# Attention A's relative scores: one read and one write per tile in place of alternating halves

## The chip, the cores and the metric

The kernel runs on one core of a Trainium2 chip. The metric is the device time of one execution in microseconds; the time of a kernel is the median of its runs. The engines are TensorE (PE, with its weight loads PEld), VectorE (DVE), ScalarE (ACT), GpSimd (POOL) and SyncE (SP, which issues nearly all DMAs here). Sixteen DMA engines move what SP issues.

## The reference

Input x is 4 x 2048 x 256, float32. Four layers follow each other: attention A with relative positions, a feed-forward block, causal attention B, and the feed-forward block again. All attention has 16 heads of 16 values. The stage in question is attention A:

```python
content_score = jnp.einsum('bhsp,bhtp->bhst', q + u, k)
pos_score = jnp.einsum('bhsp,htp->bhst', q + v, pos)
pos_score = _relative_shift(pos_score)      # pad a column, reshape to (s+1, s), drop the first row
score = (content_score + pos_score) / jnp.sqrt(jnp.float32(P))
weights = jax.nn.softmax(score, axis=-1)
out = jnp.einsum('bhst,bhtp->bhsp', weights, val)
```

The shift moves row i of the position scores by an amount that depends on i, and takes what lies beyond the diagonal from row i + 1.

## The kernel before

The batches run one after the other in a hardware loop (four passes), and within a pass the stages are separated by meetings of all engines. Attention A works on tiles of 128 query rows by all 2048 key columns: 16 heads x 16 tiles, 256 tiles a pass, 1024 in all. `in_order` unrolls four heads (G = 64 steps) into the body of a loop; all engines run the same steps s, each with its own lead.

The relative shift goes through DRAM. PE computes a tile's position scores into PSUM (`rows_of`, lines 565 and 569, banks of `rg`; `row_tail` for 128 more columns), ACT copies banks 0 to 2 (line 698) and DVE bank 3 and the tail (lines 752, 762) into `rel`, a ring of RING = 4 buffers of 128 x 2176 floats. SP writes the buffer to `rel_rows` in DRAM, a grid with a row pitch of W = 2176 floats (8,704 B), and reads it back with a row pitch of W - 1 floats (8,700 B) into `z`, a ring of 4 buffers of 128 x 2048 floats: each row then starts one float further to the left, which is the shift. DVE adds the content scores of PE (line 591) to z and takes the maxima (`score`, line 717, one instruction for each half of the columns), POOL subtracts the maximum (line 778), PE turns z in four quarters (`turn`, line 598), ACT takes the exponential into `pT` (line 690), and PE multiplies by the values (line 619).

The leads: the position scores of tile s + 9 (R_LEAD), SP's read of tile s + 6 (Z_LEAD), the score of tile s + 4 (C_LEAD), the turn of tile s + 2 (T_LEAD), the values of tile s + 1, all in step s.

SP's step of attention A (`sp_attn_a`, `step`, lines 857 to 869) runs in this order:
- `read_ready(n)`, n = s + 6: wait until PE has turned the last quarter of tile n - 4 (`t_full[3]`), which frees the buffer of z, and until tile n has been written in full (`rel_out`).
- `read_half(n, 0)` (line 822): 128 rows of 4,096 B.
- `write_half(r, 0)` (line 834), r = s + 9: wait for ACT's copy of bank 1, then write 128 rows of 4,096 B.
- `read_half(n, 1)`: 128 rows of 4,096 B.
- `write_half(r, 1)`: wait for DVE's copy of bank 3, ACT's copy of bank 2 and the tail, then write 128 rows of 4,608 B.
- `next_heads`: in some steps the loads of the next heads' q, k, position and value tiles.

Each DMA adds 16 to `rel_in` or `rel_out` of its buffer, and `moved` gives the count at which both halves have landed: 32 a tile. DVE's `score` waits for that count before its first half; ACT and DVE wait for `rel_out` before they copy into a buffer again. No consumer waits for one half alone.

Of the kernel before, what the change touches and what calls it, by code (L numbers as in the profile page):

```python
# [26 lines left out]
P = 128  # L27
# [4 lines left out]
S = 2048  # L32
NT = S // P
# [9 lines left out]
W = S + P  # L43
PAD = 16
FLAT = S * W
RING = 4
# [9 lines left out]
R_ACT = [0, 1, 2]  # L56
R_DVE = 3
R_FIRST = 3
HB = 4
NB = 2  # L60
G = HB * NT
# [5 lines left out]
OB = 4  # L67
# [30 lines left out]
def program(nc, a, out, nb=4, nh=H):  # L98

    ctx = ExitStack()  # L100
    with ctx:
        def sb(name, shape, dt=F32):
            return ctx.enter_context(nc.sbuf_tensor(name, shape, dt))
# [4 lines left out]
        def sem(name):  # L108
            return ctx.enter_context(nc.semaphore(name))
# [8 lines left out]
        rel_d = nc.dram_tensor("rel_rows", (NB, FLAT), F32).ap()  # L118
# [9 lines left out]
        rel = sb("rel", [P, RING, W])  # L128
        z = sb("z", [P, RING, S])
# [125 lines left out]
        rel_out = [sem(f"rel_out{k}") for k in range(RING)]  # L255
        rel_in = [sem(f"rel_in{k}") for k in range(RING)]
        qv_loaded = [sem("qv_loaded0"), sem("qv_loaded1")]
        tail_full = sem("tail_full")
        tail_copied = sem("tail_copied")
# [4 lines left out]
        QK_INC = 16 * 2 * len(GROUP)  # L264
# [6 lines left out]
        def settle(e):  # L271

            e.sem_inc(waited, 1)
# [257 lines left out]
        def in_order(e, b, step):  # L531

            def counts(p):
                return Counts(*(e.snap(b * (nh // HB * per) + p * per)
                                for per in (G, G // OB, 32 * G // RING, HB // NB * QK_INC, HB // NB * 16)))

            with e.Fori(0, 1) as p:
                base = counts(p)
                for s in range(-R_LEAD, 0):
                    step(p, base, s, lambda n: n >= 0)  # L540
            with e.Fori(0, GROUPS - 1) as p:
                base = counts(p)
                for s in range(G):
                    step(p, base, s, lambda n: True)
            with e.Fori(GROUPS - 1, GROUPS) as p:
                base = counts(p)
                for s in range(G):
                    step(p, base, s, lambda n: n < G)

        def moved(base, n):  # L550

            return base.moves + 32 * (n // RING + 1)

        def pe_attn_a(e, b):

# [123 lines left out]
        def act_attn_a(e, b):  # L679

            def step(p, base, s, here):

                r, t = s + R_LEAD, s + T_LEAD
                if here(t):
                    if s >= 0:

                        e.wait_ge(AA["pv_done"], base.tiles + (t - 1))
                    for q in range(4):
                        e.wait_ge(t_full[q], base.tiles + (t + 1))
                        e.activation(pT[:, t % 2, q * CH:(q + 1) * CH], rg[:, T_BANK[q], :], ACT.Exp,  # L690
                                     scale=SCALE).then_inc(p_ready[q], 1)
                if here(r):
                    if s >= 0 or r >= RING:

                        e.wait_ge(rel_out[r % RING], moved(base, r - RING))
                    for c in R_ACT:
                        e.wait_ge(r_full[c], base.tiles + (r + 1))
                        e.activation(rel[:, r % RING, c * CH:(c + 1) * CH], rg[:, R_BANK[c], :],  # L698
                                     ACT.Copy).then_inc(r_copied[c], 1)

            in_order(e, b, step)

        def dve_attn_a(e, b):

            def score(p, base, n, half, first):

                ready, read = (("lo_ready", "lo_read"), ("hi_ready", "hi_read"))[half]
                mx = (mlo, mhi)[half][:, n % 2:n % 2 + 1]
                if half == 0:
                    e.wait_ge(rel_in[n % RING], moved(base, n))  # L710
                    if not first:

                        e.wait_ge(AA["nmax_ready"], base.tiles + (n - 1))
                e.wait_ge(AA[ready], base.tiles + (n + 1))
                settle(e)
                zs = z[:, n % RING, 2 * half * CH:2 * (half + 1) * CH]
                e.tensor_tensor_reduce(out=zs, in0=scf[:, 2 * half * CH:2 * (half + 1) * CH], in1=zs, scale=1.0,  # L717
                                       scalar=-3.0e38, op0=ALU.add, op1=ALU.max, accum_out=mx).then_inc(AA[read], 1)
# [72 lines left out]
        def load_pair(e, q, k, q_src, k_src, h, groups, done):  # L791

            for i in groups:
                load_group(e, q, k, q_src, k_src, h, i, done)

        def load_v(e, h, hd, done):
            e.dma_start(v_s[hd].rearrange("p t w -> p (t w)"),
                        v_d[bass.ds(h, 1)].rearrange("a p w -> (a p) w")).then_inc(done, 16)

        def sp_attn_a(e, b):  # L800

            every = range(len(GROUP))
            load_pair(e, qv_s[0], pos_s[0], qv_d, pos_d, 0, every, qv_loaded[0])
            load_pair(e, qu_s[0], k_s[0], qu_d, k_d, 0, every, AA["qk_loaded0"])
            load_v(e, 0, 0, AA["v_loaded0"])
            load_pair(e, qv_s[1], pos_s[1], qv_d, pos_d, 1, every, qv_loaded[1])

            def read_ready(p, base, n, fresh):

                k = n % RING  # L810
                if not fresh:

                    e.wait_ge(t_full[3], e.snap(base.tiles + (n - RING + 1)))
                    settle(e)
                e.wait_ge(rel_out[k], e.snap(moved(base, n)))
                settle(e)

            def read_half(n, half):

                k, hd, i0, c0 = n % RING, n // NT % NB, n % NT * P, half * S // 2  # L820
                shifted = bass.AP(tensor=rel_d.tensor, offset=hd * FLAT + i0 * W + P - 1 + c0, ap=[[W - 1, P], [1, S // 2]])
                e.dma_start(z[:, k, c0:c0 + S // 2], shifted).then_inc(rel_in[k], 16)

            def write_half(base, n, half):

                k, hd, i0, c0, c1 = n % RING, n // NT % NB, n % NT * P, half * S // 2, (S // 2, W)[half]
                for c in ((R_DVE, R_ACT[-1]) if half else (R_ACT[1],)):
                    e.wait_ge(r_copied[c], e.snap(base.tiles + (n + 1)))
                    settle(e)
                if half:  # L830
                    e.wait_ge(tail_copied, e.snap(base.tiles + (n + 1)))
                    settle(e)
                there = bass.AP(tensor=rel_d.tensor, offset=hd * FLAT + i0 * W + c0, ap=[[W, P], [1, c1 - c0]])
                e.dma_start(there, rel[:, k, c0:c1]).then_inc(rel_out[k], 16)

            def next_heads(p, base, s, final):

                hd, at = s // NT, s % NT
                nxt = (hd + 1) % NB
                if at in (1, 3, 5) and not (final and hd + 1 >= HB):  # L840
                    if at == 1:
                        e.wait_ge(AA["hi_ready"], e.snap(base.tiles + hd * NT + C_LEAD))
                        settle(e)
                    load_pair(e, qu_s[nxt], k_s[nxt], qu_d, k_d, e.snap(p * HB + (hd + 1)), ((at - 1) // 2,),
                              AA[f"qk_loaded{nxt}"])
                if at == 7 and not (final and hd + 1 >= HB):
                    e.wait_ge(AA["pv_done"], e.snap(base.tiles + (hd * NT + V_LEAD)))
                    settle(e)
                    load_v(e, e.snap(p * HB + (hd + 1)), nxt, AA[f"v_loaded{nxt}"])
                if at in (8, 10, 12) and not (final and hd + 2 >= HB):  # L850
                    if at == 8:
                        e.wait_ge(r_full[2], e.snap(base.tiles + (hd + 1) * NT))
                        settle(e)
                    load_pair(e, qv_s[hd % NB], pos_s[hd % NB], qv_d, pos_d, e.snap(p * HB + (hd + 2)), ((at - 8) // 2,),
                              qv_loaded[hd % NB])

            def step(p, base, s, here):

                n, r = s + Z_LEAD, s + R_LEAD
                final = not here(G)  # L860
                if here(n):
                    read_ready(p, base, n, s < 0 and n < RING)
                for half in range(2):
                    if here(n):
                        read_half(n, half)
                    if here(r):
                        write_half(base, r, half)
                if s >= 0:
                    next_heads(p, base, s, final)

            in_order(e, b, step)


# [650 lines left out]
```

## Time and profile before

| | |
|---|---|
| median of 3 runs | 10,336.33 us (10,335.39 to 10,343.65) |
| the profiled execution | 10,338.86 us |
| its span, first to last instruction | 10,337.1 us |
| mean granted TensorE clock | 0.950 |
| PE, PEld busy | 8931.8 us (86%), 5887.2 us (57%) |
| DVE, ACT, POOL busy | 5900.6 us (57%), 5858.0 us (57%), 2783.3 us (27%) |
| moved by DMA | 2543.88 MB in 725600 packets, mean 246 GB/s |

The page also cuts the span into 40 slices with the busy tenths of each engine, the granted clock and the DMA engines' mean busy share, lists the costliest groups of instructions with the idle time ahead of them and what ended it, and lists the DMA issues with their sizes and the median time from issue to landing. A DMA share a little over 1 means that packets of one engine overlap a little. The trace answers the same questions for any stretch of the span.

### The profile page before, as it was taken

The numbers are of one execution on the slowest core, as the hardware profiler recorded it, in microseconds if no ns is written. First come the engines' busy times: TensorE is split into PE (matmuls) and PEld (weight loads), VectorE is DVE, ScalarE is ACT, GpSimd is POOL, SyncE is SP. The second block draws the span as 40 slices with busy tenths as digits, with TensorE's granted clock in tenths as the row PEclk, the third lists the DMA queues.
The fourth block names the chain that finished last, engine by engine and source line by source line (L and its number), as shares of the span: only waits on it lengthen the run. The fifth ranks groups of instructions, "written<-read, shape, count | busy, mean of one in ns | idle before, by whom it ended". The sixth has DMA issues, their size and how long they took to land. (4 is left out here: it accounts for less than half of the span.)

```text
span 10337.1 us, 258386 instructions
## 1 busy us (share of the span) xinstructions
PE 8931.8 (86%) x91488; PEld 5887.2 (57%) x91488; DVE 5900.6 (57%) x12492; ACT 5858.0 (57%) x10813; POOL 2783.3 (27%) x2894
## 2 busy tenths in 40 slices
PE   5888889899688888989968888898996888889899
PEld 3666666445466666644546666664554666666455
DVE  3666664564466666457446666646734666664673
ACT  3666664354466666445446666644544666664453
POOL 2333332100233333210023333321013333332101
PEclk8999999899899999989989999998998999999899
DMA  6999994110699999411069999932107999993210
GB/s 246 391 379 379 393 390 191 65 34 17 241 388 376 381 388 389 170 66 35 15 262 386 380 381 388 388 148 70 31 17 282 391 378 376 387 390 128 70 35 23
DMA packets 725600, 2543.88 MB, mean 246 GB/s; under 512 B 91521, under 2 KB 113537, under 8 KB 723969
## 3 DMA queue, kind: packets, MB, share of 16 engines
q1 hardware_dynamic: 724224, 2526.14, 64.3%
q8 instruction: 791, 12.96, 0.5%
q14 instruction: 585, 4.78, 0.1%
HBM read 1276.14 MB, written 1248.85 MB: 244 GB/s over the span
## 5 line engine op out<-in xcount | busy, mean ns | idle before, releaser
L717 DVE CUSTOM_DVE_ANT_0 z<-sc,z 128x1024 f32<-128x1024 f32 x2048 | 2497.1, 1220 | 1543.9 <-DMA z<-rel_rows 1294.4
L778 POOL TENSOR_SCALAR z<-z,nmax 128x1024 f32<-128x1024 f32 x2048 | 2274.9, 1123 | 3957.8 <-DVE nmax L727 3957.8
L690 ACT ACTIVATE pT<-rg 128x512 f32<-128x512 f32 x4096 | 2448.7, 598 | 724.5 <-PE rg L598 663.0
L598 PE MATMUL rg<-ident,z 128*128 128x128 f32 x16384 | 2535.9, 278 | 52.6 <-issue 44.6
L698 ACT ACTIVATE rel<-rg 128x512 f32<-128x512 f32 x3072 | 1722.4, 596 | 1345.4 <-PE rg L565 746.5
L598 PEld LDWEIGHTS rg<-ident,z 128*128 128x128 f32 x16384 | 1989.4, 143 | 744.3 <-ACT rel L698 290.6
L1017 ACT ACTIVATE pT<-rg 128x512 f32<-128x512 f32 (+3 forms) x2560 | 1226.1, 530 | 832.8 <-PE rg L949 502.3
L565 PE MATMUL rg<-pos_s,qv_s 96*128 96x512 bf16 (+3 forms) x2560 | 905.6, 360 | 773.4 <-DVE rel L752 770.6
L1033 DVE TENSOR_REDUCE mx_b<-sc 128x1 f32<-128x1024 f32 (+7 forms) x1024 | 1004.9, 991 | 501.9 <-PE sc L931 262.9
L619 PE MATMUL op<-pT,xnT 128*32 128x128 f32 x32768 | 1138.0, 281 | 0.0
L619 PEld LDWEIGHTS op<-pT,xnT 128*32 128x32 f32 x32768 | 851.5, 111 | 247.7 <-issue 208.6
L565 PEld LDWEIGHTS rg<-pos_s,qv_s 96*128 96x128 bf16 x2560 | 308.0, 121 | 1127.2 <-DVE rel L752 1021.7
L569 PE MATMUL rg<-pos_s,qv_s 96*128 96x512 bf16 (+3 forms) x2304 | 824.1, 362 | 102.6 <-DMA pos_s<-pos_parts 101.8
L926 PE MATMUL sc<-z 96*128 96x512 bf16 (+3 forms) x2560 | 766.0, 370 | 169.7 <-DMA z<-k_parts 96.2
L949 PE MATMUL rg<-z 99*128 99x512 bf16 (+3 forms) x2560 | 742.4, 357 | 42.9 <-issue 25.3
L752 DVE COPY rel<-rg 128x512 f32<-128x512 f32 x1024 | 702.5, 686 | 111.6 <-PE rg L569 111.6
L591 PE MATMUL sc<-k_sb,xnT 96*128 96x512 bf16 x2048 | 634.3, 392 | 0.0
L759 DVE COPY po_sb<-op 128x128 f32<-128x128 f32 x1024 | 299.0, 292 | 561.9 <-PE op L619 558.6
L591 PE MATMUL sc<-xnT 96*128 96x512 bf16 x2048 | 617.8, 383 | 0.6 <-DVE mlo L717 0.6
L1090 POOL CAST half_b<-mx_b 128x16 bf16<-128x16 f32 x64 | 12.6, 197 | 2013.1 <-DVE mx_b L1038 2013.1
L964 PE MATMUL rg<-pT,xnT 128*32 128x128 f32 x10752 | 494.0, 280 | 0.0
L926 PEld LDWEIGHTS sc<-z 96*128 96x128 bf16 x2560 | 227.4, 100 | 438.9 <-DVE mx_b L1033 156.3
(111 smaller groups left out, 9097.7 us busy)
## 6 DMA issues: line engine op xcount, KB each, us to landing
z<-rel_rows SPq DMA_DIRECT2D x2048, 512.0 KB, 7.2
rel_rows<-rel SPq DMA_DIRECT2D x1024, 576.0 KB, 7.8
rel_rows<-rel SPq DMA_DIRECT2D x1024, 512.0 KB, 6.2
v_heads<-rel SPq DMA_DIRECT2D x8, 4096.0 KB, 12.5
xnT<-v_heads SPq DMA_DIRECT2D x128, 256.0 KB, 3.2
qu_parts<-z SPq DMA_DIRECT2D x36, 512.0 KB
qv_parts<-z SPq DMA_DIRECT2D x24, 512.0 KB
k_parts<-z SPq DMA_DIRECT2D x24, 512.0 KB
```

What stands on the lines that cost most here:

```text
L565: mm = e.matmul(rg[:, R_BANK[c], 0:edge], qv_s[hd][:, i0:i0 + P], pos_b[hd][:, j0:j0 + edge], start=True, stop=True)
L569: mm = e.matmul(rg[:, R_BANK[c], edge:CH], qv_s[hd][:, i0 + 1:i0 + P + 1], pos_b[hd][:, j0:j0 + CH - edge], start=True, stop=True)
L591: mm = e.matmul(sc[:, c, :], qu_s[hd % NB][:, i0:i0 + P], k_s[hd % NB][:, c * CH:(c + 1) * CH], start=True, stop=True)
L598: mm = e.transpose(rg[:, T_BANK[q], (j - 4 * q) * P:(j - 4 * q + 1) * P], z[:, n % RING, j * P:(j + 1) * P], ident[:, :])
L619: mm = e.matmul(po[32 * g:32 * g + 32, :], v_s[hd % NB][:, j, :], pT[:, n % 2, j * P:(j + 1) * P], start=j < 4, stop=j + 4 >= NT)
L690: e.activation(pT[:, t % 2, q * CH:(q + 1) * CH], rg[:, T_BANK[q], :], ACT.Exp, scale=SCALE).then_inc(p_ready[q], 1)
L698: e.activation(rel[:, r % RING, c * CH:(c + 1) * CH], rg[:, R_BANK[c], :], ACT.Copy).then_inc(r_copied[c], 1)
L717: e.tensor_tensor_reduce(out=zs, in0=scf[:, 2 * half * CH:2 * (half + 1) * CH], in1=zs, scale=1.0, scalar=-3.0e38, op0=ALU.add, op1=ALU.ma ...
L778: e.tensor_scalar(zs, zs, 1.0, nmax[:, n % 2:n % 2 + 1], ALU.mult, ALU.add).then_inc(AA[done], 1)
L926: mm = e.matmul(scf[:, 2 * half * CH + c0 - k0:2 * half * CH + c1 - k0], q_b[n % HB][0:KROWS, s * P:(s + 1) * P], k_b[n % HB][0:KROWS, c0:c1],
L1017: e.activation(pT_b[:, i % PTS, i0 * P:CH], rg[:, i % 2, i0 * P:CH], ACT.Exp, scale=SCALE).then_inc(BB["exp_done"], 1)
L1033: e.tensor_reduce(into, scf[:, 2 * half * CH:2 * half * CH + k1 - k0], AX.X, ALU.max, negate=True).then_inc(BB["reduced"], 1)
```

## The change

Each tile's read becomes one DMA of 128 rows of 8,192 B, and its write one DMA of 128 rows of 8,704 B. The read is issued as soon as `read_ready` lets it; the write follows when the copies of banks 3 and 2 and of the tail are done (bank 1 is copied before bank 2 on the same engine). The counts go from 32 to 16 a tile. Addresses, bytes, rings, leads and all other engines' work are the same.

```diff
             def counts(p):
                 return Counts(*(e.snap(b * (nh // HB * per) + p * per)
-                                for per in (G, G // OB, 32 * G // RING, HB // NB * QK_INC, HB // NB * 16)))
+                                for per in (G, G // OB, 16 * G // RING, HB // NB * QK_INC, HB // NB * 16)))
...
-            return base.moves + 32 * (n // RING + 1)
+            return base.moves + 16 * (n // RING + 1)
...
-            def read_half(n, half):
-
-                k, hd, i0, c0 = n % RING, n // NT % NB, n % NT * P, half * S // 2
-                shifted = bass.AP(tensor=rel_d.tensor, offset=hd * FLAT + i0 * W + P - 1 + c0, ap=[[W - 1, P], [1, S // 2]])
-                e.dma_start(z[:, k, c0:c0 + S // 2], shifted).then_inc(rel_in[k], 16)
-
-            def write_half(base, n, half):
-
-                k, hd, i0, c0, c1 = n % RING, n // NT % NB, n % NT * P, half * S // 2, (S // 2, W)[half]
-                for c in ((R_DVE, R_ACT[-1]) if half else (R_ACT[1],)):
+            def read_rows(n):
+
+                k, hd, i0 = n % RING, n // NT % NB, n % NT * P
+                shifted = bass.AP(tensor=rel_d.tensor, offset=hd * FLAT + i0 * W + P - 1, ap=[[W - 1, P], [1, S]])
+                e.dma_start(z[:, k, :], shifted).then_inc(rel_in[k], 16)
+
+            def write_rows(base, n):
+
+                k, hd, i0 = n % RING, n // NT % NB, n % NT * P
+                for c in (R_DVE, R_ACT[-1]):
                     e.wait_ge(r_copied[c], e.snap(base.tiles + (n + 1)))
                     settle(e)
-                if half:
-                    e.wait_ge(tail_copied, e.snap(base.tiles + (n + 1)))
-                    settle(e)
-                there = bass.AP(tensor=rel_d.tensor, offset=hd * FLAT + i0 * W + c0, ap=[[W, P], [1, c1 - c0]])
-                e.dma_start(there, rel[:, k, c0:c1]).then_inc(rel_out[k], 16)
+                e.wait_ge(tail_copied, e.snap(base.tiles + (n + 1)))
+                settle(e)
+                there = bass.AP(tensor=rel_d.tensor, offset=hd * FLAT + i0 * W, ap=[[W, P], [1, W]])
+                e.dma_start(there, rel[:, k, :]).then_inc(rel_out[k], 16)
...
-                for half in range(2):
-                    if here(n):
-                        read_half(n, half)
-                    if here(r):
-                        write_half(base, r, half)
+                if here(n):
+                    read_rows(n)
+                if here(r):
+                    write_rows(base, r)
```

## Rows read from the trace of the kernel before

**Rows 1.** The page: span, DMA share in 40 slices (tenths), group of line 752.

```profile
span 10337.1 us, 258386 instructions
...
DMA  6999994110699999411069999932107999993210
...
L752 DVE COPY rel<-rg 128x512 f32<-128x512 f32 x1024 | 702.5, 686 | 111.6 <-PE rg L569 111.6
```

**Rows 2.** Windows of stage A: engines busy, PEclk, DMA share, GB/s.

```profile
core 0: us, PE busy (x) PEld busy (x) DVE busy (x) ACT busy (x) POOL busy (x), PEclk, DMA share, GB/s
...
200.00:1500.00 1300.00, 1127.67 (x13110) 816.55 (x13110) 825.50 (x1865) 873.82 (x1540) 488.74 (x440) 0.98 1.01 387
```

**Rows 3.** Groups of instructions by line, 600 to 1300 us.

```profile
L717 DVE CUSTOM_DVE_ANT_0 z<-sc,z 128x1024 f32<-128x1024 f32 x238 | 290.3, 1220 | 174.3 <-DMA z<-rel_rows 141.9 <-PE sc L591 32.3
...
L565 PE MATMUL rg<-pos_s,qv_s 96*128 96x512 bf16 (+1 forms) x301 | 107.0, 360 | 84.3 <-DVE rel L752 83.9
...
L752 DVE COPY rel<-rg 128x512 f32<-128x512 f32 x119 | 81.6, 686 | 0.0
```

**Rows 4.** Timeline of one tile: start us, us, engine, line.

```profile
1203.93 0.60 PE L598 MATMUL rg<-ident,z 128*128 128x128 f32 x4
...
1204.71 0.32 SPq L822 DMA_DIRECT2D z<-rel_rows  x1
...
1207.45 0.32 SPq L834 DMA_DIRECT2D rel_rows<-rel  x1
...
1207.82 0.42 SPq L822 DMA_DIRECT2D z<-rel_rows  x1
...
1208.83 0.42 SPq L834 DMA_DIRECT2D rel_rows<-rel  x1
```

**Rows 5.** DMA issues of the page and the view of issues: count, KB, us to landing.

```profile
z<-rel_rows SPq DMA_DIRECT2D x2048, 512.0 KB, 7.2
rel_rows<-rel SPq DMA_DIRECT2D x1024, 576.0 KB, 7.8
...
xnT<-v_heads SPq DMA_DIRECT2D x128, 256.0 KB, 3.2
...
qv_s<-qv_parts SPq DMA_DIRECT2D x64, 192.0 KB, 6.2
...
qv_s<-qv_parts SPq DMA_DIRECT2D x64, 128.0 KB, 5.7
...
qv_s<-qv_parts SPq DMA_DIRECT2D x64, 64.0 KB, 5.2
...
rel<-in_embT SPq DMA_DIRECT2D x1, 2048.0 KB, 11.8
```

**Rows 6.** SP's waits of 600 to 1300 us; landings of line 822, then of line 834.

```profile
SPq L273 <- ACT rel L698: 206.1, 219, 3.6
SPq L273 <- PE rg L598: 124.7, 81, 3.7
...
DMA to landing us min/median/max: 3.4/7.2/10.1
...
DMA to landing us min/median/max: 2.8/7.1/10.7
```

**Rows 7.** Windows at the start, weights and then embT alone.

```profile
6.00:7.00 1.00, 0.00 (x0) 0.00 (x0) 0.00 (x0) 0.00 (x0) 0.00 (x0) 1.00 1.04 363
18.00:22.00 4.00, 0.00 (x0) 0.00 (x0) 0.00 (x0) 0.00 (x0) 0.00 (x0) 1.00 1.02 421
21.00:22.00 1.00, 0.00 (x0) 0.00 (x0) 0.00 (x0) 0.00 (x0) 0.00 (x0) 1.00 1.02 426
```

**Rows 8.** Single windows in stage A, of 3 us and of 1 us.

```profile
239.00:242.00 3.00, 3.00 (x45) 2.27 (x34) 0.70 (x3) 2.08 (x4) 2.23 (x2) 1.00 1.04 426
850.00:853.00 3.00, 3.00 (x46) 2.16 (x47) 1.77 (x5) 1.87 (x4) 1.41 (x2) 1.00 1.02 419
1093.00:1094.00 1.00, 1.00 (x9) 0.68 (x7) 0.12 (x1) 0.86 (x2) 0.00 (x0) 1.00 0.97 304
```

## The prediction

> **What bounds the kernel now.** I read the page first for where the DMA engines are full. The table of 40 slices shows four equal passes; in each the DMA share stands at nine tenths or more for about six slices and then falls to one or none [rows 1]. Those six slices are Attention A; everything after them moves little. The change touches this stage alone, 256 tiles in a pass, 1024 in all: the page counts 1024 COPY instructions of line 752, one a tile, in a span of 10,337.1 us [rows 1].
>
> Next come the windows of the stage. From 200 to 1500 us the DMA share is 1.01 at 387 GB/s, while PE is busy 1127.67 of 1300 us (0.87) at a granted clock of 0.98, 2.4 GHz for nearly all of it [rows 2]. The groups of 600 to 1300 us show 119 tiles in 700 us, so one tile takes 5.88 us [rows 3]. DVE stands idle 141.9 us there for the DMA of z, 1.19 us a tile; PE's stall of 83.9 us on line 565 waits for the copy of line 752, which stands behind that score on DVE [rows 3]. So the chain is: read of z lands, DVE scores, DVE copies, PE goes on. Without the wait PE needs 0.87 x 5.88 = 5.1 us a tile; that is the next bound, 0.77 us lower. In bytes a tile moves 128 x 8,192 read and 128 x 8,704 written, 2.163 MB, and beside it the loads of a head: four tensors in pieces of 192, 128 and 64 KB and 256 KB of values, 1792 KB, 0.115 MB a tile [rows 5]; 2.278 MB at 387 GB/s is 5.89 us, which is the period. The stage is bound by DMA bytes, and neither count of bytes changes.
>
> The timeline of one tile shows the order [rows 4]. PE's fourth turn starts at 1203.93 and ends at 1204.53; SP issues the read of the first half at 1204.71, then waits for ACT's copy of bank 1, issues the first write half at 1207.45, the second read half only then, at 1207.82, and the last write half at 1208.83. So the second read half leaves 3.1 us after the ring has a place for it.
>
> **The change part by part.**
>
> Half as many issues. Four a tile become two. An issue costs SP 0.32 to 0.43 us [rows 4], so 0.7 us of SP's time a tile goes. SP waits 206.1 + 124.7 us in 700 [rows 6], 2.8 us a tile, so this is off the path: nothing gained.
>
> The whole read leaves at once. 3.1 us earlier for its second half in the tile shown. In a stage whose DMA engines are full, a read that is queued earlier is not served earlier for good: the ring opens the next read only when tile n-4 has been turned, and the rate stays the bytes' rate. I count nothing for it. What would be late next, were the rate higher, is PE at 5.1 us.
>
> The whole write leaves later, behind the copies of banks 2 and 3 and the tail: its first half 1.4 us later (1207.45 to 1208.83). Behind the waiting SP stand the head loads of the same step and the read of the next tile; the last write half waited for the same three counters before, so none of these is held longer. Who waits for the write: the read of that tile, three steps later (3 x 5.88 = 17.6 us after the read gate of the write's step; less the 4.1 us at which the write is issued, 13.5 us are left, against landings of 7.1 us in the median and 10.7 at most [rows 6]), and the copies of ACT and DVE into the ring four tiles on. Cost nothing as long as landings stay under 13.5 us.
>
> Half as many packets. Per tile 512 become 256, on each of 16 engines 32 become 16. What one packet costs beyond its bytes is not in a row; windows of nearly pure streams bound it. The load of embT is the last of the start, 2048 KB in rows of 8,192 B, landing 11.8 us after its issue [rows 5, 7]; at some 425 GB/s it takes 4.9 us, so the windows between 18 and 22 us are it: 421 GB/s over all four, 426 in the last, on one engine 26.6 B/ns, 308 ns a packet [rows 7]. The weights before it have rows of 1,024 B, best window 363 GB/s, 45.1 ns a packet [rows 7]. The line through both has 36.6 ns a KB (1,000 B) and 7.6 ns at zero: the upper end, as the small-packet windows also hold other stalls. The lower end is zero: within stage A single windows of 3 us reach 419 and 426 GB/s with packets of 4,096 and 4,608 B [rows 8], as much as the 8,192 B stream. As the stage's own windows are the nearer rows, I take 3 ns, under the middle. 16 x 3 = 48 ns a tile, 49 us in all; ends 0 and 16 x 7.6 = 122 ns, 125 us.
>
> Stalls of the stage. The mean of 387 against about 421 GB/s in clean windows is 5.88 x (1 - 387/421) = 0.47 us a tile, 486 us in all, in which packets take longer than their bytes (a window of 304 GB/s at a share of 0.97 lies among those of 419 and 426 [rows 8]). Whether such a stall costs by time or by packet no row shows. I take by time: unchanged.
>
> Sum: the profiled execution took 10,338.86 us (span 10,337.1 and 1.8 around it). 10,338.9 - 49 = 10,290. The median of the three runs is 2.5 us below the profiled time, so 10,287 us.
>
> **A rule of the Trainium skill.** Stage A's rows read off the grid: each starts 8,700 B after the last, so hardly one starts at a multiple of 256 B, and yet the best windows of the stage equal those of the aligned embT stream [rows 7, 8]. "DMA: Bandwidth & Descriptors", section "How a descriptor splits into AXI transactions", says that a descriptor that doesn't start on 256 B first fetches from the boundary below. By that rule, two halves touch 34 pieces and a whole row 33, one piece less in each of 8 rows an engine; the trace speaks against its full price. As a mechanism of this kernel it is the third rival.
>
> **The rivals.**
> - The stalls go by packet. Then merging halves them for 2.163 of 2.278 MB: 0.47 x 0.95 / 2 = 0.22 us a tile, 230 us more: 10,057. For it: 8,192 B packets ran at 421 GB/s over 18:22 [rows 7], stalls included, against 387 in the stage. Against it: that was four microseconds of reads without writes beside them. The tile would take 5.6 us, still above PE's 5.1. Chance 0.15.
> - Nothing happens: the cost of a packet is hidden behind the one before it, and the earlier read is worth nothing because the engines are full. 10,336. For it: equal best windows [rows 7, 8]. Chance 0.18.
> - Misaligned reads lose one 256 B piece a row: 8 x 256 B / 26.6 B/ns = 77 ns a tile, 79 us more than the forecast: 10,208. Chance 0.05.
> - Slower: the queue runs dry before the write. Place: between the read's issue and the write's, which were 4.1 us apart in the tile shown with two other issues between them. Now only the read lies there: 2.6 us of work (1.049 MB at 400 GB/s). What is queued ahead of it must cover 1.5 us. Landings of read halves are 7.2 us in the median against 3.4 at least [rows 6], so 3.8 us are queued ahead in the median tile, and it decides only in tiles where a landing comes in under 4.9 us. A hole is at most 1.5 us; in one tile of ten (my estimate, from the distance of least and median) that is 0.15 us a tile, 154 us: 10,287 + 154 = 10,441. The same total could come from coarser turns of reads and writes at the memory, if they lengthen the stalls by a third (486 / 3 = 162 us). Against it: the read that leaves 3.1 us earlier fills the queue by as much. Chance 0.22.
>
> **How the numbers follow.** Forecast 10,287, chance 0.40, its own range 10,210 to 10,320 (packets at 7.6 ns, and at nearly nothing). Eight in ten: down to 10,050, which takes in the first rival, and up to 10,390, half of the slower one's price; beyond lie about 0.05 below and 0.12 above. A measurement of this kernel can tell about 0.2%, 21 us, from no change. Faster by more than that: 0.32 of the forecast's 0.40, 0.15 and 0.05: 0.52. Within: 0.08 and 0.18, 0.26. Slower: 0.22.
>
> **What would show it.** In the profile after: packets fall by 262,144; windows of 200 to 1500 us at a share still about 1.0 and 390 GB/s instead of 387; tiles every 5.83 us; DVE's wait for z stays above 1.1 us a tile. If stalls go by packet, those windows show over 400 GB/s and DVE's wait falls by about 0.25 us a tile. If the queue runs dry, the DMA share falls below 0.98 there and the GB/s with it, with the wait of DVE for z longer. The write's landing should stay below 13.5 us; were it more, SP's wait for rel_rows would appear. I am wrong if the stage's rate moves by more than 2% either way while the share stays 1.0: then the stalls depend on the order or size of transfers, which I counted at nothing.

## The result, and the profile after

The changed kernel takes 10,138.75 us in the median (10,130.16 to 10,169.46, 4 runs) beside 10,339.99 us for the kernel before (10,335.39 to 10,344.36, 4 runs): a ratio of 0.9814, 95% interval 0.9802 to 0.9826. It is 201 us faster. I had forecast 10,287 us, 49 us faster; the measured time lies inside my range of eight in ten, but outside the forecast's own range and more than four times the gain.

The page of the kernel after: its span, the DMA share in 40 slices, the packets of the whole core, and the queue of the DMAs that SP issues (packets, MB, share of 16 engines' span).

```profile
span 10139.0 us, 255314 instructions
...
DMA  6999994110699999321069999932107999992110
...
DMA packets 430659, 2543.52 MB, mean 251 GB/s; under 512 B 58752, under 2 KB 80768, under 8 KB 166912
...
q1 hardware_dynamic: 429312, 2526.01, 63.4%
```

The same bytes move in 429,312 packets; before it was the line below.

```profile
q1 hardware_dynamic: 724224, 2526.14, 64.3%
```

262,144 of the 294,912 packets that are gone are the merged halves (256 a tile), the other 32,768 are completions: two DMAs a tile less, 16 engines each. The share times the span is the time that an engine's packets took, added up: 0.643 x 10,337.1 = 6,647 us before, 0.634 x 10,139.0 = 6,428 us after, 219 us less with the same bytes (the share is given to 0.1%, some 10 us). That is about the whole gain, but it explains nothing yet: where the share stands at 1.0, the time of the packets is the time of the stage.

The window of stage A that answers to [rows 2]:

```profile
200.00:1500.00 1300.00, 1160.36 (x13555) 840.92 (x13554) 851.47 (x1928) 900.14 (x1588) 503.79 (x454) 0.98 1.00 399
```

The stage moves 399 GB/s instead of 387, 3.1% more, at a share of 1.00 and the same mean granted clock, 0.98 of 2.4 GHz. The groups of 600 to 1300 us, for [rows 3]:

```profile
L717 DVE CUSTOM_DVE_ANT_0 z<-sc,z 128x1024 f32<-128x1024 f32 x246 | 300.0, 1220 | 159.0 <-DMA z<-rel_rows 125.4 <-PE sc L591 33.6
...
L565 PE MATMUL rg<-pos_s,qv_s 96*128 96x512 bf16 (+2 forms) x302 | 106.3, 357 | 67.5 <-DVE rel L752 67.2
...
L752 DVE COPY rel<-rg 128x512 f32<-128x512 f32 x123 | 84.4, 686 | 0.0
```

123 tiles instead of 119, 5.69 us a tile. DVE's wait for z is 125.4 us, 1.02 us a tile instead of 1.19, and PE's wait on line 565 0.55 instead of 0.71. The order within one tile, for [rows 4], and the landings of the page, for [rows 5]:

```profile
1208.16 0.60 PE L598 MATMUL rg<-ident,z 128*128 128x128 f32 x4
...
1208.93 0.32 SPq L822 DMA_DIRECT2D z<-rel_rows  x1
...
1212.36 0.32 SPq L833 DMA_DIRECT2D rel_rows<-rel  x1
```

```profile
rel_rows<-rel SPq DMA_DIRECT2D x1024, 1088.0 KB, 8.8
z<-rel_rows SPq DMA_DIRECT2D x1024, 1024.0 KB, 9.3
```

The turn's last quarter ends at 1208.16 + 0.60; the whole read leaves 0.17 us later, and the write 3.4 us after the read. The read is under way for 9.3 us in the median, longer than a half read took before (7.2), yet DVE waits less for it. The second half of its columns now leaves with the first.

### The profile page after: what moved, and what is told of

Read it like the earlier page. It is cut to its first block and busy times, and to the rows that moved or that the text cites. A ratio compares the mean times of both kernels' runs of the same rounds, so it can differ in the third digit from the quotient of the medians.

```text
span 10139.0 us, 255314 instructions
## 1 busy us (share of the span) xinstructions
PE 8886.4 (88%) x91488; PEld 5859.4 (58%) x91488; DVE 5898.7 (58%) x12492; ACT 5848.5 (58%) x10813; POOL 2784.1 (27%) x2894
## 3 DMA queue, kind: packets, MB, share of 16 engines
q1 hardware_dynamic: 429312, 2526.01, 63.4%
```

## The experiments

All were timed beside the kernel before on the same chip, in five rounds (half_read in three). The ratios are to it; times in us are medians. Where a difference of two ratios is turned into us below, it is multiplied by 10,337. The table has the runs that only change how a tile's read and write are cut and when they leave; the others stand in their sections.

| kernel | reads | writes | ratio (95%) | median |
|---|---|---|---|---|
| changed kernel | 1, at once | 1, after all copies | 0.9814 (0.9802-0.9826) | 10,138.75 |
| halves_new_order | 2, at once | 2, after all copies | 0.9883 (0.9868-0.9898) | 10,214.61 |
| halves_read_first | 2, at once | 2, as before | 0.9901 (0.9886-0.9916) | 10,235.83 |
| whole_reads | 1, at once | 2, as before | 0.9838 (0.9825-0.9852) | 10,167.97 |
| whole_writes | 2, at once | 1, after all copies | 0.9861 (0.9846-0.9876) | 10,188.19 |
| late_less | 1, after bank 3 | 1 | 0.9836 (0.9822-0.9849) | 10,160.69 |
| late_read | 1, after bank 1 | 1 | 1.0273 (1.0250-1.0295) | 10,617.23 |
| write_first | 1, after the write | 1 | 1.1200 (1.1175-1.1225) | 11,591.30 |

**The order alone.** The change did three things at once, and each could be the cause. Packet theory: half as many packets. Order theory: the whole read leaves at once, and the write after it. Transfer theory: two DMAs a tile instead of four. The first run keeps the halves and takes over only the new order.

halves_new_order:

```diff
-                for c in ((R_DVE, R_ACT[-1]) if half else (R_ACT[1],)):
+                for c in (() if half else (R_DVE, R_ACT[-1])):
...
-                if half:
+                if not half:
                     e.wait_ge(tail_copied, e.snap(base.tiles + (n + 1)))
...
-                for half in range(2):
-                    if here(n):
-                        read_half(n, half)
-                    if here(r):
-                        write_half(base, r, half)
+                if here(n):
+                    read_half(n, 0)
+                    read_half(n, 1)
+                if here(r):
+                    write_half(base, r, 0)
+                    write_half(base, r, 1)
```

> The issue order and the waits of the changed kernel (both reads as soon as the ring allows, then both writes after the copies of banks 3 and 2 and the tail), but each transfer still in two halves of 4,096 and 4,096 or 4,608 B. Packet theory (the gain of 201 us goes by the number of packets, their own cost and the stalls with them): about 10,340 us, stage A at 387 GB/s as before. Order theory (the gain comes from the read that leaves at once and from longer turns of reads and of writes): 10,140 to 10,200 us, 398 GB/s or more. Transfer theory (it goes by the number of DMAs, four to two a tile): 10,340 us.

halves_read_first has only the second part of that diff; the writes keep their waits.

> Only the reads are moved: both halves of the read leave at once, the first write half still leaves after the copy of bank 1 and the last after the other copies; all four transfers stay. Packet theory and transfer theory: 10,340 us. Order theory: 10,140 to 10,200 us, if the early read is what matters; 10,340 us, if the long turns of writes are.

Measured: 0.9883 and 0.9901. None of the three theories holds alone. The order gives 0.0117 x 10,337 = 121 us of the 192 us that the ratio 0.9814 stands for (201 us by the medians of the first comparison), and most of it (0.0099, 102 us) comes with the reads alone. The page of halves_new_order:

```profile
span 10195.4 us, 257362 instructions
...
q1 hardware_dynamic: 724224, 2526.14, 64.3%
...
z<-rel_rows SPq DMA_DIRECT2D x2048, 512.0 KB, 8.1
```

```profile
200.00:1500.00 1300.00, 1137.47 (x13382) 824.08 (x13382) 840.95 (x1904) 890.62 (x1571) 497.02 (x449) 0.99 1.01 394
```

The packets are those of the kernel before to the last one, 724,224, and yet they took 0.643 x 10,195.4 = 6,556 us an engine instead of 6,647, at 394 GB/s instead of 387.

**Pieces that were no pieces.** The changed kernel with each row cut in two, then in four, by a third dimension of the access pattern (shown for the read; the write is cut the same way; ... marks what is left out of a line).

```diff
-                shifted = ... ap=[[W - 1, P], [1, S]])
-                e.dma_start(z[:, k, :], shifted) ...
+                shifted = ... ap=[[W - 1, P], [S // 2, 2], [1, S // 2]])
+                e.dma_start(z[:, k, :].rearrange("p (a c) -> p a c", a=2), shifted) ...
```

> The changed kernel with two DMAs a tile, but each row cut in the access pattern into two pieces, 4,096 B in the read and 4,352 B in the write: 512 packets a tile as before the change. Packet theory: 10,310 to 10,340 us. Order theory and transfer theory: 10,140 to 10,190 us, with at most 49 us for packets by the price I had forecast.

> As two_pieces with four pieces a row, 2,048 and 2,176 B: 1024 packets a tile, 48 a DMA engine more than in the changed kernel. Packet theory, price in proportion (201 us for 16 packets a tile and engine): 10,139 + 3 x 201 = 10,740 us. Order and transfer theory with my forecast's 3 ns a packet: 10,139 + 48 x 3 ns x 1024 = 10,286 us.

Measured: 10,147.84 us (0.9811) and 10,139.34 us (0.9812). They tell nothing of packets: the pieces of a row lie next to each other on both sides, and the queue of four_pieces has no packet more than the changed kernel's, so they were moved as one.

```profile
q1 hardware_dynamic: 429312, 2526.01, 63.3%
```

What they are is two repeats of the changed kernel; the three ratios lie within 0.0003.

**Which merge carries the rest.** From halves in the new order (0.9883) to whole transfers (0.9814) there are 0.0069, 71 us. whole_reads merges only the read and whole_writes only the write; each keeps one counter at 32 a tile and sets the other to 16. From the diff of whole_reads:

```diff
-                shifted = ... offset=hd * FLAT + i0 * W + P - 1 + c0, ap=[[W - 1, P], [1, S // 2]])
-                e.dma_start(z[:, k, c0:c0 + S // 2], shifted) ...
+                shifted = ... offset=hd * FLAT + i0 * W + P - 1 + c0, ap=[[W - 1, P], [1, S]])
+                e.dma_start(z[:, k, :], shifted) ...
...
-                for half in range(2):
-                    if here(n):
-                        read_half(n, half)
-                    if here(r):
-                        write_half(base, r, half)
+                if here(n):
+                    read_half(n, 0)
+                if here(r):
+                    write_half(base, r, 0)
+                    write_half(base, r, 1)
```

> Only the read is one DMA of 8,192 B rows, issued at once; the writes stay in two halves that leave as in the kernel before. Packet theory, with halves_read_first at ratio 0.990 as its base and half of the packets merged: ratio 0.986 (8 of 16 packets). If only reads stall and stalls go by packet, nearly all of the rest comes here: 0.982.

> The other half of whole_reads: reads in two halves of 4,096 B that leave at once, the write whole (8,704 B rows) after all copies; three DMAs a tile. If reads and writes share the price of packets and DMAs evenly: between halves_new_order (0.988) and the changed kernel (0.981), ratio 0.985. If only reads carry it: 0.988.

Measured: 0.9838 and 0.9861. Merging the reads gives 0.0063 over halves_read_first and 0.0047 over whole_writes, 65 and 49 us; merging the writes 0.0024 (whole_reads to the changed kernel, which also holds the write's first half back) and 0.0022 (halves_new_order to whole_writes), 25 and 23 us. The reads carry about two thirds. For the writes the intervals of the kernels compared touch or overlap, so their third is less certain.

**Packets or transfers.** row_halves has whole rows but takes even and odd rows apart, four DMAs a tile in the new order. The read (the write is cut the same way):

```diff
-                shifted = ... offset=... + P - 1 + c0, ap=[[W - 1, P], [1, S // 2]])
-                e.dma_start(z[:, k, c0:c0 + S // 2], shifted) ...
+                shifted = ... offset=... + P - 1 + p0 * (W - 1), ap=[[2 * (W - 1), P // 2], [1, S]])
+                e.dma_start(z[slice(p0, P, 2), k, :], shifted) ...
```

> The order of the changed kernel, packets of whole rows (8,192 and 8,704 B, 256 a tile as in it), but four DMAs a tile as in the kernel before: each transfer is cut by rows, even and odd ones. Two earlier runs of the same call's kind had the order alone at ratio 0.988 to 0.990 and the whole change at 0.981; what is left, 75 to 90 us, goes by packets or by DMAs. Packet theory: ratio 0.981 to 0.983. Transfer theory (each DMA's completion packets and start cost it): ratio 0.988.

Measured: 0.9858 (0.9843 to 0.9873), 10,189.29 us: between the two theories. Its packets took less time than those of halves_new_order (0.635 x 10,185.0 = 6,467 us against 6,556):

```profile
span 10185.0 us, 257362 instructions
...
q1 hardware_dynamic: 462080, 2526.14, 63.5%
```

But its issues are dearer. The write's issues, min/median/max in ns, in the changed kernel, in halves_new_order and in row_halves:

```profile
L833 SPq DMA_DIRECT2D rel_rows<-rel x1024: 319/320/1738, 167.7 to 9177.0; - x171
```

```profile
L834 SPq DMA_DIRECT2D rel_rows<-rel x2048: 319/382/1671, 169.8 to 9231.8; - x187
```

```profile
L835 SPq DMA_DIRECT2D rel_rows<-rel x2048: 471/567/1586, 168.9 to 9223.6; - x187
```

An issue takes 567 ns for half the rows, against 320 for all of them. Two issues in a row alone account for little of it: halves_new_order has them too, and takes 382 (for the reads, 450 against 595 in row_halves). The next run pressed on that, with four DMAs of every fourth row each way.

> As row_halves, but eight DMAs a tile of 32 rows each: packets and bytes of the changed kernel. row_halves (four DMAs) had 10,189 us against 10,139 for two: 25 us for each DMA more a tile. Transfer theory, in proportion: 10,290 us. If the 50 us of row_halves are no price of a DMA (rows of every second partition, a chance of the order): 10,190 us.

Measured: 1.0780 (1.0766 to 1.0795), 11,145.72 us, far beyond the proportion. SP's timeline shows why: it issues almost without a pause, a DMA every 0.69 to 0.71 us (the issue itself has a median of 0.59), and of SP's waits 0.4 us are left between 600 and 1300 us.

```profile
999.89 2.76 SPq L835 DMA_DIRECT2D rel_rows<-rel  x4
1002.83 2.83 SPq L823 DMA_DIRECT2D z<-rel_rows  x4
1006.34 1.11 SPq L835 DMA_DIRECT2D rel_rows<-rel  x2
```

So a new bound, SP itself, is what this run measures, and not the price of a transfer on the DMA engines. The split of the 71 us between packets and transfers stays open. row_halves lies 50 us over the changed kernel and, with the same number of DMAs as halves_new_order and a slower SP, 25 us under it; that suggests at least 25 us for the packets, but the intervals of the two overlap. "DMA: Bandwidth & Descriptors" in the Trainium skill, section "Rules for kernel authors", says not to cut a transfer into halves by partitions, as the halves share the same DMA engines; the run agrees that nothing is gained by it, with 50 us lost here.

**The lead of the read.** Three runs let the read leave later and keep every packet as in the changed kernel. write_first issues the write ahead of the read; late_read lets the read wait for ACT's copy of bank 1 (below), and late_less for DVE's copy of bank 3 (`R_DVE` in place of `R_ACT[1]`).

```diff
+                if here(n) and here(r):
+                    e.wait_ge(r_copied[R_ACT[1]], e.snap(base.tiles + (r + 1)))
+                    settle(e)
                 if here(n):
                     read_rows(n)
```

> The changed kernel with its two DMAs swapped in each step: the write first, then the read, which so leaves some 4 us after the ring has room for it. Transfers, packets and bytes are the changed kernel's. If the order's part of the gain comes from the early read (the queues of the DMA engines don't run dry and the ring has slack): time is lost, 10,250 us and up, DMA share under 0.99. If it comes from long turns of reads and of writes in place of alternating halves: about 10,140 us, no change.

> The changed kernel, whole transfers, but the read also waits for ACT's copy of bank 1, as the second read half did in the kernel before; the read still goes ahead of the write. If the order's part of the gain (100 to 125 us of 201) is the read's lead: it is lost, and more as the whole read is late: 10,250 to 10,400 us, DMA share below 1.00. If it was the longer turns of reads and writes alone: 10,140 us.

> As late_read, but the read waits for DVE's copy of bank 3 instead of ACT's of bank 1: some 1.3 us behind the room in the ring instead of 2.6 us, by the timelines. Lead theory (each part of a us that the read leaves later costs more than the one before: 0 at the start, 478 us at 2.6 us): 10,200 to 10,300 us. If the loss has a threshold between the two: 10,140 us.

Measured: write_first 11,591.30, late_read 10,617.23, late_less 10,160.69 us. One tile of late_read and one of late_less (the turn's last quarter, SP's issues):

```profile
1206.58 0.60 PE L598 MATMUL rg<-ident,z 128*128 128x128 f32 x4
...
1210.10 0.33 SPq L822 DMA_DIRECT2D z<-rel_rows  x1
...
1211.43 0.33 SPq L833 DMA_DIRECT2D rel_rows<-rel  x1
```

```profile
1206.25 0.60 PE L598 MATMUL rg<-ident,z 128*128 128x128 f32 x4
...
1207.62 0.33 SPq L822 DMA_DIRECT2D z<-rel_rows  x1
```

In late_read the read leaves 2.9 us after the quarter's end, in late_less 0.8 us (I had expected 1.3). These are single tiles; their neighbours show 2.7 us, and 0.6 and 0.9 us. In write_first a read left 6.7 us after it (1203.96 to 1210.64). The windows of stage A, in the order late_less, late_read, write_first:

```profile
200.00:1500.00 1300.00, 1154.90 (x13519) 836.97 (x13517) 850.61 (x1923) 898.41 (x1585) 502.15 (x453) 0.99 1.00 398
```

```profile
200.00:1500.00 1300.00, 1090.60 (x12626) 790.06 (x12625) 795.18 (x1796) 842.12 (x1481) 468.92 (x423) 0.98 0.99 372
```

```profile
200.00:1500.00 1300.00, 1028.67 (x10788) 741.06 (x10792) 680.21 (x1535) 726.50 (x1268) 402.55 (x363) 0.89 0.87 318
```

The row of late_read matters most. It has the bytes and packets of the changed kernel and a DMA share of 0.99, and moves 372 GB/s instead of 399. Its page:

```profile
span 10579.3 us, 256326 instructions
...
q1 hardware_dynamic: 429312, 2526.01, 64.5%
```

0.645 x 10,579.3 = 6,824 us of packet time for the 429,312 packets that took 6,428 in the changed kernel. Packets last longer when the read leaves late, and the share then stays near 1.0 although the stage is slower. It is no mean over full stretches and holes: cut into 1,300 windows of 1 us, the stage has a share below 0.8 in 20 of them in the kernel before, in 21 in the changed kernel and in 29 in late_read, but in 260 in write_first. Sorted by the time since the last read was issued, the windows of late_read have 357 and 342 GB/s in the fourth and fifth us, at shares of 1.02 and 0.99; those of the changed kernel have 413 and 406. Of these three runs only write_first lets the share itself fall, to 0.87, and there PE's mean granted clock falls too, to 0.89 in the stage, between its levels of 2.4 and 1.2 GHz.

The loss is 22 us at some 0.8 us of delay (the intervals of late_less and of the changed kernel just touch, so it may be nothing), 478 at 2.9, 1,453 at 6.7: it grows faster than the delay. I had expected at most 10,400 us of late_read and at least 10,200 of late_less; the first lost more, and the second came nearer to the value for a threshold. One rival stands beside the delay. A late read also leaves closer to the write: from the read to the next write the median is 3.2 us in the changed kernel, 2.9 in late_less and 1.3 in late_read, and in write_first the read leaves 0.4 us after the write. No run changes the one without the other, so whether the delay or the closeness makes the packets last longer is not shown.

Does more lead than the changed kernel's help? loads_early issues the next heads' loads between the read and the write, so that they no longer stand ahead of the next read (its diff is below); early_half is whole_writes with the first read half released by the second quarter's turn instead of the fourth's.

```diff
                 if here(n):
                     read_rows(n)
+                if s >= 0:
+                    next_heads(p, base, s, final)
                 if here(r):
                     write_rows(base, r)
-                if s >= 0:
-                    next_heads(p, base, s, final)
```

> The changed kernel with the next heads' loads issued between a step's read and its write, in the time in which SP waits for the copies, instead of after the write, where their issue (1.9 us in one step) holds up the next read by 0.4 us or more in the steps that have them. If the read's lead counts even now: 10,080 to 10,120 us. If the stage is bound by bytes once the read leaves at once: 10,140 us.

> As whole_writes, but the first read half leaves when the second quarter of the tile four back has been turned, about 1.5 us before there is room for the second half. If more lead than the changed kernel's still helps: faster than whole_writes by 30 us or more. If the lead is enough once the read leaves at once, as loads_early suggests: within 15 us of whole_writes.

Measured: 10,140.53 us (0.9806, 0.9793 to 0.9820), the same as the changed kernel; and 10,213.10 us (0.9888, 0.9872 to 0.9903), 28 us worse than whole_writes by the ratios, which neither case of its expectation allowed for. More lead than the changed kernel's gained nothing in either run; why early_half loses isn't shown.

**Alignment.** Rows are read from a multiple of 256 B, with the write's own pitch. The kernel leaves out the relative shift, and moves the same bytes.

```diff
-                shifted = ... offset=hd * FLAT + i0 * W + P - 1, ap=[[W - 1, P], [1, S]])
+                shifted = ... offset=hd * FLAT + i0 * W, ap=[[W, P], [1, S]])
```

> The changed kernel, but the read takes each row from its first float with a pitch of 8,704 B instead of 8,700 B: every packet starts at a multiple of 256 B; the relative shift is left out, so the scores are others, and the same bytes are moved. If a misaligned start costs a 256 B piece a row: at least 40 us less than the changed kernel, about 10,060 to 10,100 us. If it costs nothing, as I read the windows of the kernel before: 10,140 us.

Measured: 10,149.05 us (0.9822, 0.9809 to 0.9836), the same as the changed kernel within the intervals; the window of the stage:

```profile
200.00:1500.00 1300.00, 1149.76 (x13524) 833.58 (x13523) 851.58 (x1924) 898.58 (x1586) 502.04 (x453) 0.99 1.00 398
```

A misaligned start costs nothing that shows here, to some 20 us. The rule that I had weighed, in the Trainium skill's page "DMA: Bandwidth & Descriptors", section "How a descriptor splits into AXI transactions", shows no price in this kernel.

**The next bound.** half_read shows what limits the stage once it moves fewer bytes. It leaves out the read of each row's second half.

```diff
-                shifted = ... ap=[[W - 1, P], [1, S]])
-                e.dma_start(z[:, k, :], shifted) ...
+                shifted = ... ap=[[W - 1, P], [1, S // 2]])
+                e.dma_start(z[:, k, 0:S // 2], shifted) ...
```

> The changed kernel reading only the first 1024 columns of each row back; the second half of z keeps what was there, so the scores of those columns are left wrong, and a tile moves 1.75 instead of 2.28 MB. Shows the next bound: my forecast had PE at 5.1 us a tile against 5.7 us now, so 10,139 - 0.6 x 1024 = 9,540 us, with DVE's wait for z gone and the DMA share near 0.8; if the stage is bound by something else than bytes, it stays above 9,900 us.

Measured: 9,698.92 us (0.9385, 0.9370 to 0.9399). Groups and window:

```profile
L717 DVE CUSTOM_DVE_ANT_0 z<-sc,z 128x1024 f32<-128x1024 f32 x266 | 324.5, 1220 | 116.4 <-PE sc L591 116.4
...
L752 DVE COPY rel<-rg 128x512 f32<-128x512 f32 x133 | 91.2, 686 | 0.0
```

```profile
200.00:1500.00 1300.00, 1244.54 (x14731) 902.34 (x14732) 925.40 (x2093) 972.74 (x1725) 545.76 (x492) 0.99 0.92 333
```

133 tiles in 700 us, 5.26 us a tile. DVE no longer waits for z but for PE's content scores. PE is busy 0.96 of the window, 5.04 us a tile, near the 5.1 that I had; what I missed is the 0.2 us in which it still waits. The share tells the same story as late_read's: I had expected it near 0.8, and it reads 0.92 with only 333 GB/s moved; at that rate a full share would be 362 GB/s, where the changed kernel moves 399.

## Why the prediction was wrong

- *The stage is bound by DMA bytes; a read that is queued earlier is not served earlier for good.* This step failed. I took a share of 1.01 for proof that the rate stays the bytes' rate whenever the transfers leave. halves_new_order has the same bytes and packets as the kernel before and is 121 us faster; late_read has the same bytes and packets as the changed kernel, a share of 0.99, and is 478 us slower. The time recorded for the same packets changes with the order, so a share of 1.0 doesn't show that the engines move bytes as fast as they can. The sign of being wrong that I had named came true: the rate moved by 3.1% at a share of 1.00.
- *The whole read leaves at once: counted at nothing.* This is the term of the sum that the failed step put at nothing. With halves it is worth 121 us together with the later write, 102 us with the reads alone. That agrees in direction with late_read: in the kernel before, the second half left 3.1 us late in the tile shown [rows 4]. The same edit also takes the second read half out from between the two writes, 0.4 us behind one and 1.0 us ahead of the other in that tile, so closeness is a rival here too. Long turns of reads and writes are not enough by themselves, as late_read and write_first have them and lose, but whether they add something is not shown.
- *Half as many packets: 3 ns each, 49 us, ends 0 and 125.* The size was somewhat small: 71 us for packets and transfers together, 69 ns a tile or 4.3 ns for each of the 16 packets, inside the bounds. I had left out the two completions a tile and engine. How much of the 71 us is the packets' is open.
- *The whole write leaves later: nothing.* Right in the main: going from halves_read_first to halves_new_order the ratio moves from 0.9901 to 0.9883, within the intervals of one another. The write lands in 8.8 us in the median, below the 13.5 I allowed, but the longest took 14.7, and SP's wait for rel_rows, which I had named as the sign of it, does appear: 12 times in the whole span of the changed kernel, 18.7 us in all (the line below), none of them between 600 and 1300 us. The kernel before has no such wait.
- *Half as many issues are off the path.* Right as far as the runs go: SP waits 452 us of 700 in the changed kernel's window (below), and loads_early, which takes the loads' issue out from ahead of the next read, gains nothing. With eight issues a tile, in row_quarters, SP is the bound.
- *Stalls unchanged.* Not measured apart. Their sum with everything else that lengthens packets fell by 91 us with the order alone (6,647 to 6,556). The rival by which they go by packet had 230 us more for it; merging gave 71 us at most, so it is not borne out, though its signs (over 400 GB/s, DVE's wait 0.25 us a tile shorter) were nearly met at 399 and 0.17 and so could not have told it from the order.
- *Nothing happens.* Refuted by 201 us. It shared the failed step: the earlier read was worth nothing to it too.
- *Slower rival, queue dry before the write.* It looked at the right thing, when the transfers are queued, and had the wrong sign. A dry queue is not what the kernel before suffered from: it has no more windows at a share below 0.8 than the changed kernel (20 and 21 of 1,300). I had written that the read "fills the queue by as much" as evidence against the rival, and given it no price as a gain.
- *Misaligned reads.* Rightly given little: aligned_whole shows no price.
- *PE as the next bound at 5.1 us.* Nearly: 5.26 us measured.

SP's waits of 600 to 1300 us in the kernel after, for [rows 6]:

```profile
SPq L273 <- ACT rel L698: 301.1, 122, 4.1
SPq L273 <- PE rg L598: 140.9, 90, 5.3
SPq L273 <- DVE rel L752: 10.5, 25, 1.1
```

And from its waits in the whole span (us in all, times, longest):

```profile
SPq L273 <- DMA rel_rows<-rel: 18.7, 12, 2.6
```

Of the 192 us by the ratio (201 by the medians), 121 go to the order and 71 to merged transfers, shown by halves_new_order. How packets come to last longer when the read leaves late, whether by the delay or by its closeness to the write, and how the 71 us divide between packet size and number of DMAs, stays open. That the measured time still lay inside the range of eight in ten was in part luck: its lower end was drawn for stalls that go by packet, and not for the order.

## What to carry to other kernels

A DMA share of 1.0 doesn't show that a stage is bound by bytes; compare GB/s with the same stream's best windows, and ask how late each transfer leaves after its buffer is free. Where, as here, a ring of four buffers feeds a stage that DMA nearly fills, try issuing the read first and in one piece, with the write, which has slack, behind it; lead that is already enough gained nothing more. Before cutting a transfer by partitions, look at what its issue costs: 0.32 us became 0.57.

## What was not expected of the hardware

- The time that the same packets take depends on when their transfers are issued: 6,428 us an engine for 429,312 packets with the read at once, 6,824 with the read 2.9 us late and 1.3 us ahead of the write.
- An issue by SP of 32 or 64 rows with a step of several partitions took 0.57 to 0.60 us in the median, one of 128 rows 0.32, or 0.38 to 0.45 where two were issued in a row (halves_new_order).
- Rows of 8,192 B with a pitch of 8,700 B, hardly one of which starts at a multiple of 256 B, were read as fast as aligned ones: 10,138.75 against 10,149.05 us.
